# A one-hot row fetch on TensorE: a batch of three columns in every three groups instead of every four

## The reference

```python
for l in range(3):
    f = (nf @ W_ni[l])[src] + (nf @ W_nj[l])[dst] + ef @ W_fij[l] + bias[l]
    f = leaky_relu(f, 0.2).reshape(-1, 4, 32)
    e = einsum('ehd,hd->eh', f, attn[l])
    a = exp(e - segment_max(e, dst)[dst]);  a = a / segment_sum(a, dst)[dst]
    h = segment_sum((nf @ W_node[l]).reshape(-1, 4, 32)[src] * a[:, :, None], dst)
    nf, ef = h.mean(axis=1), f.mean(axis=1)
return x + nf            # the first nf is relu(layernorm(x))
```

## Time and profile before

| | us |
|---|---|
| median of 3 runs | 2992.46 |
| lowest, highest run | 2990.29, 3013.71 |
| span of the profiled execution, first to last instruction | 3006.7 |
| DVE busy in it | 2490.5 (83%) |
| PE busy in it | 2404.8 (80%) |
| POOL busy in it | 2058.9 (68%) |

### The profile page before, as it was taken

The page is one execution under the profiler, slowest core; times in us unless marked ns, Lnnn a source line. Parts: engine busy times, 40 slices in busy tenths (PEclk is TensorE's granted clock), DMA queues, the critical chain, the costliest instruction groups (busy, mean ns, idle before and its releaser), DMA issues.

```text
span 3006.7 us, 50077 instructions
## 1 busy us (share of the span) xinstructions
PE 2404.8 (80%) x15871; PEld 1878.0 (62%) x16027; DVE 2490.5 (83%) x6428; ACT 1447.6 (48%) x3416; POOL 2058.9 (68%) x2167
## 2 busy tenths in 40 slices
PE   3388888888887378888888887649999888998984
PEld 1366667676764356667766665337777777776753
DVE  7399999999997468998999998637888888879784
ACT  0155555555555135555556555414445454445452
POOL 6777777777770577777777776377776666667653
PEclk9699988888899589987999999857778787778796
DMA  6235454535342324343435342332333343333222
GB/s 252 64 96 156 122 147 116 152 110 158 110 128 85 112 74 142 119 149 110 157 111 158 110 153 98 118 103 67 100 120 99 98 136 98 108 108 100 91 92 81
DMA packets 139275, 353.92 MB, mean 118 GB/s; under 512 B 43895, under 2 KB 96027, under 8 KB 120207
## 3 DMA queue, kind: packets, MB, share of 16 engines
q1 hardware_dynamic: 67216, 296.09, 27.9%
q0 software_dynamic: 68960, 39.71, 8.6%
q10 hardware_dynamic: 2838, 14.91, 1.3%
HBM read 137.79 MB, written 212.77 MB: 117 GB/s over the span
## 4 chain that ended last, share of the span: by engine, by line
PE 39%; DVE 29%; issue 14%; ACT 9%; POOL 5%; DMA 3%; SPq 1%; DVEq 0%; ACTq 0%; POOLq 0%
DVE U L1349 12%; PE f_ps L695 12%; PE pick_ps L664 10%; PE f_ps L704 9%; PE xT_ps L685 5%; DVE rows L1266 4%; DVE lr L1277 4%; DVE U L1334 3%; POOL rows L554 2%; ACT f_low L850 2%; ACT xT L841 2%; ACT up L901 2%; PE f_ps L714 2%; ACT wide_ps L889 1%; DVE rows L1378 1%
## 5 line engine op out<-in xcount | busy, mean ns | idle before, releaser
L554 POOL DMA_INDIRECT rows<-nf_tab,src_sb x1995 | 1889.3, 947 | 706.9 <-issue 574.9
L704 PEld LDWEIGHTS f_ps<-w_out,lr 128*128 128x128 f32 x4836 | 701.0, 210 | 379.0 <-issue 277.3
L664 PE MATMUL pick_ps<-nf_part,z 125*128 125x160 bf16 x6345 | 630.0, 264 | 258.4 <-issue 217.0
L1349 DVE TENSOR_TENSOR_SCAN U<-wide_ps,U 128x272 f32<-128x272 f32 (+2 forms) x1272 | 801.6, 694 | 3.2 <-ACT wide_ps L889 2.4
L695 PE MATMUL f_ps<-xT,w_edge 97*128 97x512 f32 x1212 | 753.8, 708 | 22.6 <-ACT ef_new L872 12.0
L664 PEld LDWEIGHTS pick_ps<-nf_part,z 125*128 125x128 bf16 x6345 | 564.6, 112 | 289.8 <-issue 241.3
L704 PE MATMUL f_ps<-w_out,lr 128*128 128x36 f32 (+1 forms) x4836 | 649.8, 274 | 31.2 <-DVE lr L1277 28.8
L1277 DVE TENSOR_TENSOR lr<-f_ps,f_low 128x512 f32<-128x512 f32 x606 | 410.0, 677 | 252.4 <-ACT f_low L850 247.0
L850 ACT ACTIVATE f_low<-f_ps 128x512 f32<-128x512 f32 x606 | 361.0, 596 | 495.9 <-PE f_ps L695 495.9
L685 PE MATMUL xT_ps<-ident,rows 128*97 128x128 f32 x2418 | 431.8, 305 | 76.8 <-issue 37.2
L841 ACT ACTIVATE xT<-xT_ps 97x512 f32<-97x512 f32 x606 | 358.8, 592 | 147.8 <-PE xT_ps L685 145.6
(11 more groups left out here) (163 smaller groups left out, 1070.5 us busy)
## 6 DMA issues: line engine op xcount, KB each, us to landing
u_tab<-up SPq DMA_DIRECT2D x144, 1088.0 KB
s_nd<-edge_first SPq DMA_DIRECT2D x48, 768.0 KB
rows<-nf_tab,src_sb POOLq DMA_INDIRECT x1995, 2.5
ef_tab<-ef_new SPq DMA_DIRECT2D x32, 768.0 KB
ef_st<-ef_tab SPq DMA_DIRECT2D x32, 768.0 KB
z<-fifth_tab SPq DMA_DIRECT2D x141, 96.0 KB
edge_first<-s_nd ACTq DMA_DIRECT2D x16, 768.0 KB
ef_st<-in_edge_attr_dram SPq DMA_DIRECT2D x16, 672.0 KB
```

The costliest lines, as they stand in the source:

```text
L554: eng.indirect_dma_start(rows[q % RING][:, c * K:c * K + D], None, nf_tab[:, :], bass.IndirectOffsetOnAxis(ap=src_sb[:, t:t + 1], axis=0)) ...
L664: mm = eng.matmul(pick_ps[:, i * PB:(i + 1) * PB], hot[m % 2][0:NQ, f * PW + i * P:f * PW + (i + 1) * P], nf_part[a][0:NQ, f * PB:(f + 1) ...
L704: mm = eng.matmul(f_ps[n % 2][:, u * m:(u + 1) * m], lr[y][:, u * P:(u + 1) * P], w_out[l][:, 0:m], start=True, stop=True)
L1349: last = eng.tensor_tensor_scan(uh[:, c0 * w:c1 * w], dbc[h % 2][:, 0:(c1 - c0) * w], uh[:, c0 * w:c1 * w], 0.0, ALU.mult, ALU.add)
```

## The change

A batch is now three columns of three groups: column 2 of every group up to group 185. NPICK, the number of batches per layer, goes from 47 to 62 and the picked columns from 141 to 186, so the gathered ones from 665 to 620. TensorE's steady loop picks in every group. The first column of a batch is now picked behind `edges` and `scores` of its group, not ahead of them. `warm` is left in the loop's last few groups only. Batches run three ahead instead of two, and three instead of two are fetched at the beginning of a layer. VectorE's `make_hot` and `pick_rows` follow the groups of three and so fall behind another piece of the block's work each time. SP's loads of indices are spread accordingly.

```diff
+PICK_LEAD = 3
-    NPICK = END // GB + 1
+    NPICK = END // PICK + 1
...
         def picks(g):
-            return g % GB < PICK and g // GB < NPICK
+            return g < PICK * NPICK
...
+        def fifths_to(b):
+            return 8 if b < 0 else min(10 + GB * b // PICK, NPICK)
...
                         for b in range(max(SUBS * s - 2, 0), SUBS * s + 1):
                             store_u(k0 + b)
-                            if b + IDXB + 2 < NPICK:
-                                load_fifths(l, b + IDXB + 2)
+                            for m in range(fifths_to(b - 1), fifths_to(b)):
+                                load_fifths(l, m)
...
-                    for b in range(2):
+                    for b in range(PICK_LEAD):
                         for i in range(PICK):
                             pick(b, i)
                     eng.wait_ge(w_in, L * WI)
                     for g in range(-2, END - 2):
                         turn(g + 2)
-                        b, i = g // GB + 2, g % GB
-                        if g >= 0 and i < PICK and b < NPICK:
+                        b, i = g // PICK + PICK_LEAD, g % PICK
+                        picking = g >= 0 and b < NPICK
+                        if picking and i:
                             pick(b, i)
-                        elif g >= 1:
+                        elif not picking and g >= 1:
                             warm(g + 1, FILL_STEADY)
                         if g + 1 >= 0:
                             edges(g + 1)
                         if g >= 0:
                             scores(g)
+                        if picking and not i:
+                            pick(b, i)
...
                     pick_rows(1)
+                    make_hot(3)
+                    pick_rows(2)
...
-                        if g >= 0 and i == PICK - 1 and b + 3 < NPICK:
-                            pick_rows(b + 3)
-                        if g >= 0 and i == 0 and b + 4 < NPICK:
-                            make_hot(b + 4)
+                        m, at = g // PICK + PICK_LEAD, g % PICK
+                        if g >= 0 and at == PICK - 1 and m < NPICK:
+                            pick_rows(m)
+                        if g >= 0 and at == 0 and m + 1 < NPICK:
+                            make_hot(m + 1)
```

More of the change, by code:

```diff
@@ L103, in egat_kernel @@
     fix_tab = nc.dram_tensor("fix_tab", (N, UR), F32, kind="Internal").ap()
-    fifth_tab = nc.dram_tensor("fifth_tab", (PICK * NB, P), FP16, kind="Internal").ap()
+    fifth_tab = nc.dram_tensor("fifth_tab", (PICK * NPICK, P), FP16, kind="Internal").ap()
     run_tab = nc.dram_tensor("run_tab", (N + 1, 1), F32, kind="Internal").ap()
@@ L228, in egat_kernel @@
         left_f = jw[:, P:P + NP]
-        pick_src = src_sb[:, 0:NPICK * SB].rearrange(
-            "p (b g u) -> p b g u", g=GB, u=GT)[:, :, 0:PICK, 2]
+        pick_src = src_sb[:, 0:NP * GT].rearrange("p (g u) -> p g u", u=GT)[:, :, 2]
         fifth16 = [xT[a][0:HNP, 0:P // 2].bitcast(FP16) for a in range(2)]
@@ L484, in _ @@
                         eng.wait_ge(prep, 7)
-                    for b in range(IDXB + 2):
-                        load_fifths(l, b)
+                    for m in range(6):
+                        load_fifths(l, m)
                     load_first(q0)
                     load_first(q0 + 1)
+                    for m in range(6, 8):
+                        load_fifths(l, m)
                     for s in range(NS):
@@ L678, in turn @@
                         if picks(g):
-                            eng.wait_ge(picked, PARTS5 * (l * NPICK + g // GB + 1))
+                            eng.wait_ge(picked, PARTS5 * (l * NPICK + g // PICK + 1))
                         if n >= 2:
@@ L1139, in _ @@
                 eng.wait_ge(src_in, 16 * (NW + 1))
-                eng.tensor_copy(left_f.rearrange("p (b g) -> p b g", g=PICK), pick_src
-                                ).then_inc(fifth_ready, 1)
+                eng.tensor_copy(left_f, pick_src).then_inc(fifth_ready, 1)
                 eng.wait_ge(fifth_ready, 2)
@@ L1365, in pick_rows @@
                         m = l * NPICK + b
-                        s, c = divmod(b * SB + 2, SUP)
+                        s, c = divmod(b * PICK * GT + 2, SUP)
                         q = q0 + s
```

## The result

The changed kernel takes **3248.99 us** (median; 3245.99 to 3253.87), the kernel before took 3001.52 beside it (2990.29 to 3013.71): ratio **1.0791** [1.0741, 1.0841]. Against the profiled execution of before, span to span, it is 3244.7 - 3006.7 = **+238.0 us**.

A forecast was written before the change was run, and what follows sets the result against it. VectorE was taken to set the pace: +123 us of its work and +52 us of waits, all else 0, sum +175 us; against the median of 2992.5 this gave 3167 us (+5.9%), range 2980 to 3330.

The forecast's parts named there:

- VectorE's work: Compares and copies of 45 more batches on VectorE, 2.74 us each: +123 us, hidden by nothing but its own waiting.
- TensorE's work: Fourth group of a block: four products of constants go, 15 picks come; about nothing at full clock, in TensorE's slack.
- GpSimd: 135 gathers fewer, 169 us of GpSimd's time, counted as 0 since nobody waits for it beyond 12.9 us.
- SP: 45 more loads of indices, issued behind the store of a block: 0.
- the layer's beginning: A third batch fetched there, 6.0 us, covered by VectorE's 6.15 us wait for destination rows: 0; 18 us if uncovered.
- The waits: VectorE's `leaky` waits behind each batch's fetch: 171 us before, 177 x 1.26 = 223 after: +52 us.
- my setting off: Per-batch wait kept at 1.26 us: longer path behind the fetch speaks for more, VectorE's heavier load for less.
- The two ends that I kept, 0.60 and 2.24: Bounds of VectorE's waiting per batch in us, from the second and third layers; 3050 up to about 3280.
- The mechanism of the waits: TensorE idles at a batch's first pick for `pick_rows`, its clock falls, `edges` come late and `leaky` waits.
- Rival A: TensorE's clock holds and `leaky` waits no more: -48 us, 2944; 9%.
- Rival B: Every batch costs VectorE the third layer's 2.24 us of waiting: +348 us, 3341; 12%.
- Rivals C and D: C: GpSimd bounds the first two layers, -112 us, 2880, 3%. D: both sides cancel, 2992, 8%.

## Why the prediction was right, and which step was wrong

The direction, the range and the bound were right: VectorE set the pace, and the change put work on it. Forecast 3167 us, measured 3249: of the added time +175 was forecast and +238 came, span against span.

- **VectorE's work**: +123 forecast, +118.3 measured. 45 batches of 2.74 us, and in the changed kernel next to nothing hides them: 43.8 us less work gave 37.9 us.
- **TensorE's work, GpSimd, SP, the layer's beginning at 0**: they held, and TensorE's longer busy time (+112.2 us) reaches VectorE only as waits. GpSimd waits for `turn` 522.9 us instead of 117.4, and nobody missed its gathers. The wait for the destination rows still covers a layer's first batches, 39.5 us before and 23.1 after, so the third batch went into it.
- **The waits**: +52 forecast, +124.5 measured. The step that failed is "I take their mean over the layers, 1.26": a batch costs 1.79 to 1.91 us. The prediction compared rows, 7.4 us against 4.1, and then set the excess off, unpriced, against VectorE's heavier load. Its 4.1 us stopped at the first `edges`, but `leaky` waited mostly a group later, behind a row of 7.34 us on the mean, with 7.89 us of VectorE's work beside it. In the changed kernel the row didn't grow, it is 5.49 us; the work beside it fell further, to 5.20, when the batches came closer. The runs price both sides of my setting off: the load takes 44 to 57 us of waiting away, the two picks ahead of `edges` put 118.3 on. The two ends that I kept, 0.60 and 2.24, held it; that the time fell into the range is owed to their width. By the sums over the places, a batch cost 1.44 us before and costs 1.84 now: 177 x 1.84 - 135 x 1.44 = +131 us, of which some 60 are the 42 further batches and some 71 the higher price.
- **The mechanism of the waits** was half right. The clock does fall behind nearly every fetch (of 180 picks with a gap ahead of them 171 took over 1.3 us, where 1.20 is full speed), and 0.80 to 0.88 was the right guess for the stretches. But the fall alone isn't the cause that I made it. It costs what it adds to the row: constants returned 98.8 us with the long row, 15.4 with the short one, and taking them from the kernel before with VectorE's load cost nothing that shows.
- **Rival A** was wrong on both counts. The clock did not hold; and where constants held it at 0.91 to 0.93, the time was 3154, not 2944. The rule of the Trainium skill that spoke for it (page "TensorE: Matmul & The Clock Gate", section "Why this matters for your kernels") makes the drop a matter of an idle gap longer than those at a batch here. The trace doesn't agree: a gap of 2.46 us ahead of the pick stands before products at half speed (2.16 us for a pick, against 1.20 in the earlier trace rows, behind a gap of 2.23 us). **Rival B** (every batch 2.24 us, 3341) was further off than the forecast, but right that a batch would cost more; its reason, the longer path, is right only beside the work that covers it. **Rivals C and D** fell: GpSimd waits more, and nothing cancelled.

## What to carry to other kernels

When an engine waits for a fetch, price the whole row of work between the end of that wait and the result that the bounding engine wants next, and set it against the work which that engine has in between; a wait's price in the old kernel belongs to the old row and the old work beside it. Look for instructions that can move behind that result before looking at clocks: moving two picks took this change from 7.9 to 3.6% slower. And a free slot in a rhythm (the fourth group here) may be what hides a wait, so a denser rhythm is more than the sum of its work.

## What was not expected of the hardware

- Filling a wait of TensorE with products of constants, 132 times six, made the kernel before 2.4% faster, though VectorE is the bound; yet taking constants away from it (beside VectorE's load) lowered the clock from 0.853 to 0.806 and cost nothing that shows. The mean clock of a kernel doesn't tell its time.
- TensorE's idle time moved for the most part when its wait was taken away: 344.6 us less at the fetch, 254.0 us more at `edges` and `scores`, at a clock of 0.826 instead of 0.834. In the kernel before, the changed order alone moved it without changing the time.
- A compare of VectorE over one column takes 206 ns, over 384 columns 319.
